# Two graph layers and a state-space scan: the three 128x1024 instructions that end the softplus move from GpSimd to VectorE, and GpSimd's output-norm work goes behind its product 13

## The chip, the cores and the metric

The kernel runs on one core of a Trainium2 chip. The metric is the device time of one execution in microseconds (us); the figure of a kernel is the median of several executions.

## The reference, cut to what matters

There are two layers on 4096 nodes with 128 features and a dense 4096x4096 adjacency matrix `adj`. The first is a pair of graph networks: `adj @ x` and `adj @ x2`, each through three dense layers, merged, added to `x` and normalized. The second is a Mamba block on `relu(adj @ x @ gcn_w + gcn_b)`:

```python
xconv = sum((xpad[k:k + L] * conv_w[:, k] for k in range(D_CONV))) + conv_b
u = jax.nn.silu(xconv)
dbc = u @ w_xp
dt = jax.nn.softplus(dbc[:, :DT_RANK] @ w_dt + b_dt)
B = dbc[:, DT_RANK:DT_RANK + D_STATE]
C = dbc[:, DT_RANK + D_STATE:]
A = -jnp.exp(A_log)
dA = jnp.exp(dt[:, :, None] * A[None])
dBu = dt[:, :, None] * B[:, None, :] * u[:, :, None]

def step(hst, inp):
    dAt, dBut, Ct = inp
    hst = dAt * hst + dBut
    return (hst, hst @ Ct)
_, ys = lax.scan(step, jnp.zeros((D_INNER, D_STATE), h.dtype), (dA, dBu, C))
y = ys + u * D_skip
y = y * jax.nn.silu(z)
return y @ w_out
```

L is 4096, D_INNER is 256 (two halves of 128 partitions) and D_STATE is 16. The result is added to the input and normalized once more.

## The kernel before, in words

**Stage A** (the first 515 us or so) turns `adj`, multiplies it with both inputs and stores the turned matrix. The change doesn't touch it.

**The scan stage** works on eight tiles of 512 nodes. One tile's turn is a window (`window(b, ...)`, one function of that name on each engine), numbered 0 to 7 here. A window has 16 steps n, one for each of the 16 states, and two more on VectorE for what trails behind. Each engine has its own program written out in order; engines meet only at semaphores, and an engine stops at a wait. Windows 2 and 3, then 4 and 5, are two passes of a loop of two iterations.

For state n of tile b there are four pieces of work:
- ScalarE makes `dA` (two exponentials of `dt`, L678);
- `dBu` is `dtu` times row n of B. For even n VectorE makes it as `dBuV` from a spread of B in PSUM (L898). For odd n GpSimd makes it as `dBuP` from `b_sb` in SBUF (L484, "product n" in the text), once scan n-3 is done;
- VectorE scans: `hs = dA * hs + dBu` over 1026 elements (L912, "scan n"), at its step n+1;
- VectorE multiplies `hs` with the spread of C in PSUM into `pr` (L919, "pr n"), at its step n+2; TensorE sums the `pr` up in `yT` (L1147). TensorE also makes the spreads of B and C (L1134 and L1143), turns, projects, and multiplies blocks of the stored adjacency for tile b+2 (L1063).

Beside this, window b does the **front** of tile b+1 (convolution, projections, softplus) and the **tail** of tile b-1 (gate, projection, output norm). The table `AT` gives the step of each such piece.

The softplus is made as relu + log(1 + exp(-abs)) with a correction of the rounding of 1 + exp. ScalarE makes the pieces at its steps 12 and 13. VectorE makes the error `sp_a` at its step 12 (`front_spd`, L868). Then come three instructions on 128x1024 floats, all with both inputs in SBUF: `sp_r = sp_r - sp_a` (L460), `dt = dt + sp_r` (L465), `dtu = dt * u` (L468). Before the change these three are `front_dt` on GpSimd, at its steps 13, 14 and 15 (`pool_dt=13`): one behind product 13, one in front of product 15, one behind it. For tile 0 VectorE makes them itself ahead of window 0 (L943, L946, L948).

The output norm of tile b-1: VectorE takes statistics at step 11 (`tail_stats`, L880 to L889), GpSimd makes `rs2` and `nb2` (`tail_rs`, L473 and L475, 4 columns each) at its step 12, between products 11 and 13, and ScalarE applies them at step 14.

In window b+1, VectorE's first instruction (`dBuV` of state 0) waits for `dtu`, and GpSimd's product 1 waits for `dtu` and for the last scan of window b. The gate (`tail_gate`, L874) stands at VectorE's step 1 of the window.

Of the kernel before, what the change touches and what calls it, by code (L numbers as in the profile page):

```python
# [7 lines left out]
ALU = mybir.AluOpType  # L8
# [23 lines left out]
def wait(eng, sem, value):  # L32

    if not isinstance(value, int) or value > 0:
# [1 line left out]

AT = dict(pool_rs=3, pool_tail_rs=12, pool_dt=13, act_hn=4, act_hT=5, act_silu=9, act_bc=11,
          act_sp=12, act_exp=13, act_tail=14, dve_g=1, dve_bc=9, dve_sp=12, dve_gate=1, dve_tail=11, pe_tr=3,  # L40
          pe_z=7, pe_dbc=8, pe_dt=10, pe_turn=2, pe_out=9, act_b0=14, act_b1=2, act_b2=5, act_b3=9, act_ax=15, act_g=0, act_start=1, act_skip=2, act_y=4)
FILL = (1, 1, 6, 1, 0, 0, 2, 9, 12)
# [9 lines left out]
def gnn_mamba(nc, x, adj, x2, eps1, eps2, W1, b1, W2, b2, Wm, bm, gcn_w, gcn_b, ln_g, ln_b, w_in, conv_w,  # L52
# [3 lines left out]
    with ctx:  # L56
# [311 lines left out]
        def _(pool):  # L368
# [85 lines left out]
                pool.wait_ge(f_inv_dev, a + 1)  # L454
                nc.gpsimd.tensor_tensor(nb[:, :], mr[:, :], rs[:, :], ALU.mult).then_inc(f_mean_scaled, 1)

            def front_dt(a, par, step):
                if step == 0:
                    pool.wait_ge(sp_error, a + 1)
                    nc.gpsimd.tensor_tensor(sp_r[:, :, :], sp_r[:, :, :], sp_a[:, :, :], ALU.subtract)\  # L460
                        .then_inc(sp_corrected, 1)
                elif step == 1:
                    pool.wait_ge(sp_corrected, a + 1)
                    pool.wait_ge(sp_log, a + 1)
                    nc.gpsimd.tensor_tensor(dt_[par][:, :, :], dt_[par][:, :, :], sp_r[:, :, :], ALU.add).then_inc(dt_ready, 1)  # L465
                else:
                    pool.wait_ge(dt_ready, a + 1)
                    nc.gpsimd.tensor_tensor(dtu[par][:, :, :], dt_[par][:, :, :], u[par][:, :, :], ALU.mult)\  # L468
                        .then_inc(dtu_ready, 1)

            def tail_rs(b):
                pool.wait_ge(o_var_eps, b + 1)
                nc.gpsimd.tensor_tensor(rs2[:, :], ve2[:, :], neg_half[:, :], ALU.pow).then_inc(o_inv_dev, 1)  # L473
# [3 lines left out]
            def window(b, par, tail, front):  # L477
                for n in range(S):
                    if n in POOL_B:
                        pair = nB(n) // 2  # L480
                        pool.wait_ge(b_in[pair % 2], 16 * (NPB // 4 * b + pair // 2 + 1))
                        wait(pool, scanned, S * b + (n - POOL_AFTER if n >= POOL_AFTER else -1) + 1)
                        pool.wait_ge(dtu_ready, b + 1)
                        nc.gpsimd.tensor_tensor(dBu(n, par)[:, :, 1:], dtu[par][:, :, :],  # L484
                                                b_sb[pair % 2][:, nB(n) % 2:nB(n) % 2 + 1, :].to_broadcast([P, H, TILE]),
                                                ALU.mult).then_inc(dBu_by_pool, 1)
                    if front and n == AT['pool_rs']:
                        front_rs(b + 1)
                    if tail and n == AT['pool_tail_rs']:
                        tail_rs(b - 1)  # L490
                    if front and 0 <= n - AT['pool_dt'] < 3:
                        front_dt(b + 1, 1 - par, n - AT['pool_dt'])

            front_rs(0)
            stage_a_over(pool)
# [253 lines left out]
        def _(dve):  # L749
# [116 lines left out]
            def front_spd(a, par):  # L866
                dve.wait_ge(sp_one_plus, a + 1)
                nc.vector.scalar_tensor_tensor(sp_a[:, :, :], dtu[par][:, :, :], -1.0, sp_a[:, :, :], ALU.add, ALU.subtract)\  # L868
                    .then_inc(sp_error, 1)

            def tail_gate(b, par):
                dve.wait_ge(summed, S * (b + 1))
                dve.wait_ge(gate_ready, 2 * b + 2)
                nc.vector.tensor_tensor(yg[:, :, :].rearrange("p q d -> p (q d)"), yT[:, :],  # L874
                                        sz[par][:, :, :].rearrange("p q d -> p (q d)"), ALU.mult).then_inc(y_gated, 1)
# [15 lines left out]
            def window(b, par, tail, front):  # L891
                for n in range(S + 2):
                    if n < S and n not in POOL_B:
                        dve.wait_ge(B_spread, NVB * b + n - nB(n) + 1)
                        if n == 0:
                            dve.wait_ge(dtu_ready, b + 1)
                        wait(dve, scanned, S * b + n - 1)
                        nc.vector.tensor_tensor(dBuV[dve_slot(n, par)][:, :, 1:], dtu[par][:, :, :],  # L898
                                                spread_bank("B", n)[:, :].unsqueeze(1).to_broadcast([P, H, TILE]), ALU.mult)\
                            .then_inc(dBu_by_dve, 1)  # L900
                    k = n - 1
                    if 0 <= k < S:
                        dve.wait_ge(dA_ready, H * (S * b + k + 1))
                        if k in POOL_B:
                            dve.wait_ge(dBu_by_pool, NPB * b + nB(k) + 1)
                        else:
                            dve.wait_ge(dBu_by_dve, NVB * b + k - nB(k) + 1)
                        wait(dve, state_kept, S * b + k - NHS + 1)
                        wait(dve, C_multiplied, S * b + k - NHS + 1)
                        dve.wait_ge(start_set, S * b + k + 1)  # L910
                        flat = [a[:, :, :].rearrange("p h t -> p (h t)") for a in (hs[k % NHS], dA[k % NDA], dBu(k, par))]
                        nc.vector.tensor_tensor_scan(flat[0], flat[1], flat[2], zero[:, :], ALU.mult, ALU.add)\  # L912
                            .then_inc(scanned, 1)
                    k = n - 2
                    if k >= 0:
                        dve.wait_ge(C_spread, S * b + k + 1)
                        dve.wait_ge(scanned, S * b + k + 1)
                        wait(dve, summed, S * b + k - NPR + 1)
                        nc.vector.tensor_tensor(pr[k % NPR][:, :, :], hs[k % NHS][:, :, 1:],  # L919
                                                spread_bank("C", k)[:, :].unsqueeze(1).to_broadcast([P, H, TILE]), ALU.mult)\  # L920
                            .then_inc(C_multiplied, 1)
                    if tail and n == AT['dve_gate']:
                        tail_gate(b - 1, 1 - par)
                    if front:
                        if n == AT['dve_g']:
                            front_g(b + 1)
                        if n == AT['dve_bc']:
                            front_bclo(b + 1, 1 - par)
                        if n == AT['dve_sp']:
                            front_spd(b + 1, 1 - par)  # L930
                    if tail:
                        if n == AT['dve_tail']:
                            tail_stats(b - 1, 1 - par)
# [5 lines left out]
            front_bclo(0, 0)  # L939
            front_spd(0, 0)  # L940

            dve.wait_ge(sp_error, 1)
            nc.vector.tensor_tensor(sp_r[:, :, :], sp_r[:, :, :], sp_a[:, :, :], ALU.subtract).then_inc(sp_corrected, 1)  # L943
            dve.wait_ge(sp_corrected, 1)
            dve.wait_ge(sp_log, 1)
            nc.vector.tensor_tensor(dt_[0][:, :, :], dt_[0][:, :, :], sp_r[:, :, :], ALU.add).then_inc(dt_ready, 1)  # L946
            dve.wait_ge(dt_ready, 1)
            nc.vector.tensor_tensor(dtu[0][:, :, :], dt_[0][:, :, :], u[0][:, :, :], ALU.mult).then_inc(dtu_ready, 1)  # L948
            dve.wait_ge(zeroed, 2 + NDA)
            window(0, 0, False, True)  # L950
            window(1, 1, True, True)
# [337 lines left out]
```

## Time and profile before

| what | value |
|---|---|
| median of 3 executions | 1172.0 us (1171.23 to 1174.01) |
| the profiled execution's own time | 1173.02 us |
| its span | 1171.5 us |
| VectorE (DVE) busy | 1053.3 us, 90% |
| TensorE (PE) busy | 1000.2 us, 85% |
| ScalarE (ACT) busy | 514.9 us, 44% |
| GpSimd (POOL) busy | 336.1 us, 29% |
| granted TensorE clock, mean of the span | 0.938 |

How to read it: the profile is one execution. Its span goes from the first to the last instruction, and its own time lies 1.5 us above that. An engine's busy time counts the time from an instruction's start to its end, also where the instruction stands still inside that time, so a stalled instruction looks like work. In a timeline row the first number is the start in us from the span's start, the second the length in us; what stands in square brackets is the engine's idle time before it and what ended it. Neighbours on VectorE overlap by about a tenth of a us, so what an instruction takes of the engine is the distance from its start to the next start.

### The profile page before, as it was taken

The numbers are of one execution on the slowest core, as the hardware profiler recorded it, in microseconds if no ns is written. First come the engines' busy times: TensorE is split into PE (matmuls) and PEld (weight loads), VectorE is DVE, ScalarE is ACT, GpSimd is POOL, SyncE is SP. The second block draws the span as 40 slices with busy tenths as digits, with TensorE's granted clock in tenths as the row PEclk, the third lists the DMA queues.
The fourth block names the chain that finished last, engine by engine and source line by source line (L and its number), as shares of the span: only waits on it lengthen the run. The fifth ranks groups of instructions, "written<-read, shape, count | busy, mean of one in ns | idle before, by whom it ended". The sixth has DMA issues, their size and how long they took to land. (4 is left out here: it accounts for less than half of the span.)

```text
span 1171.5 us, 13291 instructions
## 1 busy us (share of the span) xinstructions
PE 1000.2 (85%) x4162; PEld 691.5 (59%) x4162; DVE 1053.3 (90%) x864; ACT 514.9 (44%) x914; POOL 336.1 (29%) x207
## 2 busy tenths in 40 slices
PE   2789999999999999999988979889889798684565
PEld 1567776767777777444645646546556465463454
DVE  5899999999999998723999999999999999999994
ACT  3334334333334332225555655636456446565331
POOL 5100101000000001002354273463642734627340
PEclk9999999999999999999998989999989899895766
DMA  9989999999999999846444253253441542101100
GB/s 260 250 176 323 319 319 335 321 327 316 340 301 348 303 334 285 163 179 260 155 168 152 79 198 144 85 194 138 158 166 55 197 143 73 37 20 54 36 10 10
DMA packets 190907, 226.37 MB, mean 193 GB/s; under 512 B 8624, under 2 KB 164336, under 8 KB 176528
## 3 DMA queue, kind: packets, MB, share of 16 engines
q1 hardware_dynamic: 107008, 165.69, 44.2%
q10 hardware_dynamic: 80768, 52.70, 18.1%
q0 software_dynamic: 3088, 7.47, 2.3%
q8 instruction: 18, 0.29, 0.1%
q14 instruction: 25, 0.20, 0.1%
HBM read 162.66 MB, written 63.18 MB: 193 GB/s over the span
## 5 line engine op out<-in xcount | busy, mean ns | idle before, releaser
L771 DVE STREAM_TRANSPOSE at<-rows 128x1024 f32<-128x1024 f32 x136 | 267.2, 2005 | 24.9 <-DMA rows<-in_adj 14.2
L976 PE MATMUL yT<-ah,xh 128*128 128x512 f32 x512 | 214.4, 419 | 52.9 <-DVE al L779 52.9
L484 POOL TENSOR_TENSOR dBuP<-dtu,b_sb 128x1024 f32<-128x1024 f32 x64 | 167.2, 2613 | 256.8 <-DVE hs L912 193.8
L525 ACT ACTIVATE ah<-at 128x2048 fp32r<-128x2048 f32 x64 | 122.4, 1913 | 241.3 <-PE yT L976 231.1
L1063 PE MATMUL bank<-adjc,xm 128*128 128x512 f32 x448 | 213.6, 606 | 0.8 <-ACT axT L589 0.8
L976 PE MATMUL yT<-al,xh 128*128 128x512 f32 x512 | 202.0, 394 | 0.0
L976 PE MATMUL yT<-ah,xl 128*128 128x512 f32 x512 | 201.9, 394 | 0.0
L1147 PE MATMUL yT<-ident,pr 128*128 128x128 f32 x1024 | 159.3, 309 | 23.5 <-DVE pr L919 23.4
L912 DVE TENSOR_TENSOR_SCAN hs<-dA,zero,dBuP 128x1026 f32<-128x1026 f32 x64 | 166.3, 2598 | 8.4 <-ACT dA L678 8.4
L678 ACT ACTIVATE dA<-dt,A_sb 128x512 f32<-128x512 f32 x256 | 169.5, 713 | 9.2 <-POOL dt L465 6.5
L1147 PEld LDWEIGHTS yT<-ident,pr 128*128 128x128 f32 x1024 | 141.4, 162 | 48.8 <-DVE pr L919 33.2
L919 DVE TENSOR_TENSOR pr<-hs,bank 128x1024 f32<-128x1024 f32 x128 | 152.7, 1198 | 8.5 <-PE bank L1143 8.2
L912 DVE TENSOR_TENSOR_SCAN hs<-dA,zero,dBuV 128x1026 f32<-128x1026 f32 x64 | 157.8, 2466 | 1.6 <-DVE dBuV L898 1.2
L976 PEld LDWEIGHTS yT<-ah,xh 128*128 128x128 f32 x512 | 97.6, 191 | 88.0 <-DVE al L779 64.3
L779 DVE TENSOR_TENSOR al<-at,ah 128x2048 fp32r<-128x2048 f32 x64 | 144.3, 2254 | 0.2
L1063 PEld LDWEIGHTS bank<-adjc,xm 128*128 128x128 f32 x448 | 82.2, 197 | 71.1 <-issue 70.0
L976 PEld LDWEIGHTS yT<-ah,xl 128*128 128x128 f32 x512 | 97.7, 191 | 23.9 <-issue 5.0
L976 PEld LDWEIGHTS yT<-al,xh 128*128 128x128 f32 x512 | 97.5, 190 | 21.4
L1143 PE MATMUL bank<-bc,sel 128*128 128x512 f32 x128 | 87.1, 680 | 26.9 <-DVE pr L919 24.5
L428 POOL TENSOR_TENSOR ve<-mv,eps_ln 128x4 f32<-128x4 f32 x8 | 1.6, 195 | 326.8 <-DVE mv L796 326.8
L898 DVE TENSOR_TENSOR dBuV<-dtu,bank 128x1024 f32<-128x1024 f32 x64 | 77.8, 1215 | 1.7 <-issue 1.1
L671 ACT ACTIVATE state<-hs 128x2 f32<-128x2 f32 x128 | 25.7, 201 | 111.5 <-DVE hs L912 108.3
(147 smaller groups left out, 1027.1 us busy)
## 6 DMA issues: line engine op xcount, KB each, us to landing
adjT<-at SPq DMA_DIRECT2D x56, 1024.0 KB, 7.7
adjc<-adjT SPq DMA_DIRECT2D x56, 1024.0 KB, 5.1
rows<-in_adj SPq DMA_DIRECT2D x152, 256.0 KB, 8.6
rows<-in_adj ACTq DMA_DIRECT2D x136, 256.0 KB, 8.7
b_sb<-b_dram ACTq DMA_DIRECT2D x32, 512.0 KB, 3.8
xm<-in_x SPq DMA_DIRECT2D x4, 512.0 KB, 15.3
xs<-in_L_gnn_x SPq DMA_DIRECT2D x4, 512.0 KB, 14.7
res<-in_x POOLq DMA_DIRECT2D x8, 256.0 KB, 7.6
```

Of the source, the lines that this page charges most:

```text
L484: nc.gpsimd.tensor_tensor(dBu(n, par)[:, :, 1:], dtu[par][:, :, :], b_sb[pair % 2][:, nB(n) % 2:nB(n) % 2 + 1, :].to_broadcast([P, H, TILE ...
L525: nc.scalar.activation(ah[c % 2][:, :], at[c % 2][:, :, :].rearrange("p m t -> p (m t)"), ACT.Copy)\
L678: nc.scalar.activation(dA[n % NDA][:, h, 1:], dt_[par][:, h, :], ACT.Exp, scale=A_sb[:, h, n:n + 1]).then_inc(dA_ready, 1)
L771: last = nc.vector.transpose(dst.rearrange("p m (g i) -> p g m i", i=32), src.rearrange("p g (i m) -> p g m i", i=32))
L779: nc.vector.tensor_tensor(al[c % 2][:, :], at[c % 2][:, :, :].rearrange("p m t -> p (m t)"), ah[c % 2][:, :], ALU.subtract).then_inc(chunk ...
L898: nc.vector.tensor_tensor(dBuV[dve_slot(n, par)][:, :, 1:], dtu[par][:, :, :], spread_bank("B", n)[:, :].unsqueeze(1).to_broadcast([P, H, ...
L912: nc.vector.tensor_tensor_scan(flat[0], flat[1], flat[2], zero[:, :], ALU.mult, ALU.add)\
L919: nc.vector.tensor_tensor(pr[k % NPR][:, :, :], hs[k % NHS][:, :, 1:], spread_bank("C", k)[:, :].unsqueeze(1).to_broadcast([P, H, TILE]), ...
L976: last = mm(acc[k][:, :], w[:, b, :], v[c % 2][:, cols], start=(b == 0 and j == 0), stop=(b == KB - 1 and j == 2))
L1063: last = mm(accB[:, :], xm[:, b, :], adjc[c % NADJ][:, m, :], start=(b == 0), stop=(b == KB - 1))
L1143: mm(spread_bank("C", n)[:, :], sel[:, S + n:S + n + 1].to_broadcast([P, P]), bc[par][:, :], start=True, stop=True).then_inc(C_spread, 1)
L1147: m = mm(yT[:, DI * q + P * h:DI * q + P * h + P], src[:, h, P * q:P * q + P], ident[:, :], is_transpose=True, start=first and h == 0 and ...
```

## The change

Three edits:
- `front_dt` moves from GpSimd to VectorE, with its three instructions, waits and semaphores as they were. It stands at VectorE's steps 14, 15 and 16 (`dve_dt=14`), behind `pr` of that step.
- GpSimd's `tail_rs` goes from step 12 to step 13 (`pool_tail_rs=13`), that is from in front of product 13 to behind it.
- For tile 0, VectorE's own three instructions are now the same function; their order and waits are the same.

```diff
-AT = dict(pool_rs=3, pool_tail_rs=12, pool_dt=13, act_hn=4, act_hT=5, act_silu=9, act_bc=11,
+AT = dict(pool_rs=3, pool_tail_rs=13, dve_dt=14, act_hn=4, act_hT=5, act_silu=9, act_bc=11,
...
-            def front_dt(a, par, step):
-                if step == 0:
-                    pool.wait_ge(sp_error, a + 1)
-                    nc.gpsimd.tensor_tensor(sp_r[:, :, :], sp_r[:, :, :], sp_a[:, :, :], ALU.subtract)\
-                        .then_inc(sp_corrected, 1)
-                elif step == 1:
-                    pool.wait_ge(sp_corrected, a + 1)
-                    pool.wait_ge(sp_log, a + 1)
-                    nc.gpsimd.tensor_tensor(dt_[par][:, :, :], dt_[par][:, :, :], sp_r[:, :, :], ALU.add).then_inc(dt_ready, 1)
-                else:
-                    pool.wait_ge(dt_ready, a + 1)
-                    nc.gpsimd.tensor_tensor(dtu[par][:, :, :], dt_[par][:, :, :], u[par][:, :, :], ALU.mult)\
-                        .then_inc(dtu_ready, 1)
...
-                    if front and 0 <= n - AT['pool_dt'] < 3:
-                        front_dt(b + 1, 1 - par, n - AT['pool_dt'])
...
+            def front_dt(a, par, step):
+                if step == 0:
+                    dve.wait_ge(sp_error, a + 1)
+                    nc.vector.tensor_tensor(sp_r[:, :, :], sp_r[:, :, :], sp_a[:, :, :], ALU.subtract).then_inc(sp_corrected, 1)
+                elif step == 1:
+                    dve.wait_ge(sp_corrected, a + 1)
+                    dve.wait_ge(sp_log, a + 1)
+                    nc.vector.tensor_tensor(dt_[par][:, :, :], dt_[par][:, :, :], sp_r[:, :, :], ALU.add).then_inc(dt_ready, 1)
+                else:
+                    dve.wait_ge(dt_ready, a + 1)
+                    nc.vector.tensor_tensor(dtu[par][:, :, :], dt_[par][:, :, :], u[par][:, :, :], ALU.mult).then_inc(dtu_ready, 1)
...
+                        if 0 <= n - AT['dve_dt'] < 3:
+                            front_dt(b + 1, 1 - par, n - AT['dve_dt'])
```

**GpSimd at the end of window 1.** The rows go from the norm's two small instructions to the last instruction of the window. Each product is a row that writes `dBuP0` (product 13) or `dBuP1` (product 15). Before:

```order
L473 TENSOR_TENSOR rs2<-ve2,neg_half 128x4
L475 TENSOR_TENSOR nb2<-mr2,rs2 128x4
L484 TENSOR_TENSOR dBuP0<-dtu1,b_sb1 128x2x512
L460 TENSOR_TENSOR sp_r<-sp_r,sp_a 128x1024
L465 TENSOR_TENSOR dt0<-dt0,sp_r 128x1024
L484 TENSOR_TENSOR dBuP1<-dtu1,b_sb1 128x2x512
L468 TENSOR_TENSOR dtu0<-dt0,u0 128x1024
```

and now:

```order
L470 TENSOR_TENSOR dBuP0<-dtu1,b_sb1 128x2x512
L459 TENSOR_TENSOR rs2<-ve2,neg_half 128x4
L461 TENSOR_TENSOR nb2<-mr2,rs2 128x4
L470 TENSOR_TENSOR dBuP1<-dtu1,b_sb1 128x2x512
```

Product 13 no longer stands behind the two norm instructions, and product 15 no longer behind `sp_r` and `dt`.

**VectorE at the end of window 1**, from `sp_a` to the last `pr`. Rows that write `hs0` to `hs3` are scans 12 to 15; rows that write `pr3`, `pr0`, `pr1`, `pr2`, `pr3` are pr 11 to 15. Before:

```order
L868 SCALAR_TENSOR_TENSOR sp_a<-dtu0,sp_a 128x1024
L912 SCALAR_TENSOR_TENSOR hs0<-dA0,zero,dBuV0 128x1026
L919 TENSOR_TENSOR pr3<-hs3,bank5 128x1024
L898 TENSOR_TENSOR dBuV1<-dtu1,bank6 128x2x512
L912 SCALAR_TENSOR_TENSOR hs1<-dA1,zero,dBuP0 128x1026
L919 TENSOR_TENSOR pr0<-hs0,bank5 128x1024
L912 SCALAR_TENSOR_TENSOR hs2<-dA2,zero,dBuV1 128x1026
L919 TENSOR_TENSOR pr1<-hs1,bank6 128x1024
L912 SCALAR_TENSOR_TENSOR hs3<-dA3,zero,dBuP1 128x1026
L919 TENSOR_TENSOR pr2<-hs2,bank5 128x1024
L919 TENSOR_TENSOR pr3<-hs3,bank6 128x1024
```

and now, from scan 13 on:

```order
L908 SCALAR_TENSOR_TENSOR hs1<-dA1,zero,dBuP0 128x1026
L915 TENSOR_TENSOR pr0<-hs0,bank5 128x1024
L858 TENSOR_TENSOR sp_r<-sp_r,sp_a 128x1024
L908 SCALAR_TENSOR_TENSOR hs2<-dA2,zero,dBuV1 128x1026
L915 TENSOR_TENSOR pr1<-hs1,bank6 128x1024
L862 TENSOR_TENSOR dt0<-dt0,sp_r 128x1024
L908 SCALAR_TENSOR_TENSOR hs3<-dA3,zero,dBuP1 128x1026
L915 TENSOR_TENSOR pr2<-hs2,bank5 128x1024
L865 TENSOR_TENSOR dtu0<-dt0,u0 128x1024
L915 TENSOR_TENSOR pr3<-hs3,bank6 128x1024
```

One of the three stands behind each of pr 12, pr 13 and pr 14. What comes before scan 13 is as it was. ScalarE, TensorE and the DMA queues keep their order.

## Rows read from the trace of the kernel before

**Rows 1.** The page: busy time, share of the span, instructions, by engine.
```profile
PE 1000.2 (85%) x4162; PEld 691.5 (59%) x4162; DVE 1053.3 (90%) x864; ACT 514.9 (44%) x914; POOL 336.1 (29%) x207
```
**Rows 2.** Waits of VectorE, 515 to 1172 us: total us, times, longest us.
```profile
DVE hs L912 <- ACT dA L678: 8.4, 7, 1.5
DVE pr L919 <- PE bank L1143: 8.2, 16, 1.1
```
**Rows 3.** Timeline of VectorE, end of window 2 and start of window 3.
```profile
755.60 2.39 DVE L868 SCALAR_TENSOR_TENSOR sp_a<-dtu,sp_a 128x1024 f32<-128x1024 f32 x1
757.91 2.34 DVE L912 TENSOR_TENSOR_SCAN hs<-dA,zero,dBuV 128x1026 f32<-128x1026 f32 x1
760.18 1.19 DVE L919 TENSOR_TENSOR pr<-hs,bank 128x1024 f32<-128x1024 f32 x1
761.29 1.21 DVE L898 TENSOR_TENSOR dBuV<-dtu,bank 128x1024 f32<-128x1024 f32 x1
762.42 2.34 DVE L912 TENSOR_TENSOR_SCAN hs<-dA,zero,dBuP 128x1026 f32<-128x1026 f32 x1
...
765.80 3.28 DVE L912 TENSOR_TENSOR_SCAN hs<-dA,zero,dBuV 128x1026 f32<-128x1026 f32 x1
769.00 1.19 DVE L919 TENSOR_TENSOR pr<-hs,bank 128x1024 f32<-128x1024 f32 x1
771.34 4.37 DVE L912 TENSOR_TENSOR_SCAN hs<-dA,zero,dBuP 128x1026 f32<-128x1026 f32 x1 [1.15 <-ACT dA L678]
775.63 2.32 DVE L919 TENSOR_TENSOR pr<-hs,bank 128x1024 f32<-128x1024 f32 x2
777.87 1.21 DVE L898 TENSOR_TENSOR dBuV<-dtu,bank 128x1024 f32<-128x1024 f32 x1
779.37 2.36 DVE L912 TENSOR_TENSOR_SCAN hs<-dA,zero,dBuV 128x1026 f32<-128x1026 f32 x1 [0.29 <-DVE dBuV L898]
781.64 1.20 DVE L874 TENSOR_TENSOR yg<-yT,sz 128x1024 f32<-128x1024 f32 x1
```
**Rows 4.** Timeline of GpSimd, the same stretch.
```profile
752.32 2.24 POOL L475 TENSOR_TENSOR nb<-mr,rs 128x4 f32<-128x4 f32 x1
754.52 2.38 POOL L484 TENSOR_TENSOR dBuP<-dtu,b_sb 128x1024 f32<-128x1024 f32 x1
758.07 4.35 POOL L460 TENSOR_TENSOR sp_r<-sp_r,sp_a 128x1024 f32<-128x1024 f32 x1 [1.16 <-DVE sp_a L868]
762.50 4.43 POOL L465 TENSOR_TENSOR dt<-dt,sp_r 128x1024 f32<-128x1024 f32 x1
766.88 4.36 POOL L484 TENSOR_TENSOR dBuP<-dtu,b_sb 128x1024 f32<-128x1024 f32 x1
771.19 2.37 POOL L468 TENSOR_TENSOR dtu<-dt,u 128x1024 f32<-128x1024 f32 x1
```
**Rows 5.** Timeline of VectorE, the three instructions for tile 0, first two.
```profile
537.44 1.22 DVE L943 TENSOR_TENSOR sp_r<-sp_r,sp_a 128x1024 f32<-128x1024 f32 x1
538.70 1.22 DVE L946 TENSOR_TENSOR dt<-dt,sp_r 128x1024 f32<-128x1024 f32 x1
```
**Rows 6.** Timeline of VectorE, window 0's `sp_a` and window 1's gate.
```profile
600.99 1.21 DVE L868 SCALAR_TENSOR_TENSOR sp_a<-dtu,sp_a 128x1024 f32<-128x1024 f32 x1
...
625.65 1.20 DVE L874 TENSOR_TENSOR yg<-yT,sz 128x1024 f32<-128x1024 f32 x1
```
**Rows 7.** Timeline of VectorE, scans 12 and 13 of window 7.
```profile
1136.19 3.45 DVE L912 TENSOR_TENSOR_SCAN hs<-dA,zero,dBuV 128x1026 f32<-128x1026 f32 x1
...
1141.81 2.48 DVE L912 TENSOR_TENSOR_SCAN hs<-dA,zero,dBuP 128x1026 f32<-128x1026 f32 x1
```
**Rows 8.** Timeline of TensorE, the last wait of window 4.
```profile
931.00 0.79 PE L1134 MATMUL bank<-bc,sel 128*128 128x512 f32 x1 [4.38 <-DVE pr L919]
```
**Rows 9.** Timeline of VectorE, pr 0 and pr 1 of window 5.
```profile
942.28 1.22 DVE L919 TENSOR_TENSOR pr<-hs,bank 128x1024 f32<-128x1024 f32 x1 [0.18 <-PE bank L1143]
...
946.82 1.22 DVE L919 TENSOR_TENSOR pr<-hs,bank 128x1024 f32<-128x1024 f32 x1 [1.06 <-PE bank L1143]
```
**Rows 10.** Stretches of 2 us: us, PE busy, granted clock, DMA share, GB/s.
```profile
932.00:934.00 2.00, 2.00 (x12) 0.50 0.00 0
```

More of the change, by code:

```diff
@@ L940, in _ @@
             front_spd(0, 0)
[L942 to L948, printed above, removed]
+            for step in range(3):
+                front_dt(0, 0, step)
             dve.wait_ge(zeroed, 2 + NDA)
```

## The prediction

> **What bounds the kernel now.** I read the page first, then VectorE's waits, then the timelines of VectorE and GpSimd side by side over one window's end, and TensorE's timeline last. The page gives VectorE 90% and GpSimd 29% [rows 1]. By that alone the change is wrong: it puts 21 instructions (three in each of windows 0 to 6) on the fullest engine and takes them from an idle one. VectorE hardly waits in the scan stage either; the two largest entries that come back from window to window are 8.4 us and 8.2 us [rows 2]. So VectorE bounds this stage, and the question is whether its busy time is work.
>
> It isn't. In the timeline the same scan takes 2.34 us, then 3.28 us, then 4.37 us [rows 3]. Put GpSimd's rows beside them [rows 4]. Its `dt` starts at 762.50, while scan 13 runs from 762.42 to 764.76, and is 4.43 us long: 764.76 plus 2.17 is its end, 766.93. Scan 14 starts at 765.80; 766.93 plus 2.15 is 769.08, its end. Product 15 starts at 766.88 and lasts 4.36 us: 769.08 plus 2.16 is its end, 771.24. Then scan 15 starts at 771.34 just behind `dtu` (771.19 to 773.56) and ends at 775.71, 2.15 us behind `dtu`. The reading that fits all four: a scan (two inputs in SBUF) and a GpSimd instruction on SBUF exclude each other, the later one stands still until the other is through, and both show the standstill as busy time. VectorE's `pr` and `dBuV` (one input in PSUM) run beside GpSimd unharmed: 1.19 and 1.21 us [rows 3] while `sp_r` is on. `sp_a`, again with two SBUF inputs, is 2.39 us long where product 13 (754.52 to 756.90) is still running [rows 3, 4], and 1.21 us in window 0, where the norm work that delays product 13 doesn't exist [rows 6].
>
> The 1.15 us of idle time ahead of scan 15 are put down to ScalarE's `dA`, but scan 15 also needs product 15, which ended at 771.24, 0.1 us ahead of the start [rows 3, 4]. I take it for the releaser. It is late because `sp_r` and `dt` stand in front of it.
>
> **The change part by part.**
>
> *Three instructions on VectorE.* Alone, `sp_r` on VectorE is 1.22 us long [rows 5]. What it takes of the engine I read from `dBuV`, as long (1.21) and followed by the next start after 762.42 - 761.29 = 1.13 us [rows 3]. The bound above is 1.26 us, the distance in tile 0, where each waits for the one before [rows 5]; in the window each has a scan and a `pr` in between, so its own wait is long over. The bound below is 1.11 us, a `pr` [rows 3]. 1.13 it is.
>
> *The stretch from `sp_a` to the gate.* Before, in window 2, it is 781.64 - 755.60 = 26.04 us [rows 3]. After, I add distances between starts: `sp_a` and the three moved ones 4 x 1.13 = 4.52; scans 12 to 15, 4 x 2.27 (760.18 - 757.91) = 9.08; pr 11 to 15, 5 x 1.11 (761.29 - 760.18) = 5.55; `dBuV` 14, 1.13; the next window's first `dBuV`, 1.50, since the scan behind it waits for it (779.37 - 777.87); that scan, 2.27. Together 24.05 us.
>
> *New collisions.* Product 15 now waits only for scan 12, which ends as pr 11 starts. From there to scan 13 it has 1.11 + 1.13 = 2.24 us and needs 2.38. Window 7 shows the price of just this meeting: scan 13 is 2.48 us instead of 2.34 [rows 7], 0.14 more. Product 1 of the next window waits for `dtu`, now made behind pr 14; it has 1.11 + 1.50 us until the next scan, so 0 to 0.15, and I take 0.1. The stretch is then 24.3 us and saves 1.74 us. Windows 1 to 6 have this shape: 6 x 1.74 = 10.4 us. The four moved starts of waiting instructions are covered: `sp_error` and `sp_log` are made before scan 12, and behind `dtu` only pr 15 stands, then `dBuV`, whose input is through.
>
> *Window 0* has no norm work, so `sp_a` isn't held: 625.65 - 600.99 = 24.66 us [rows 6], less 24.3 = 0.4 us saved.
>
> *`tail_rs` behind product 13.* Product 13 waits only for scan 10, which ends before the statistics on VectorE; its 2.38 us lie beside them and `dBuV` 12. That is what frees `sp_a` above. In window 7 there is no `sp_a`, and it is scan 12 that product 13 holds: 3.45 us against 2.34 [rows 7], so 1.1 us saved. `rs2` and `nb2` wait for VectorE's `ve2` as before and end when they did (754.56 in window 2 [rows 4]); ScalarE's norm doesn't see it. `nb2` stands still through scan 11 in both orders. Product 15, queued behind it now, isn't due until 760.2. Cost 0. Tile 0's function is the same code: 0. ScalarE's first `dA` of the next window needs `dt`, now made behind pr 13 and some 7 us ahead of the scan that uses it: 0.
>
> *What TensorE gives back.* At a window's end TensorE waits 4.38 us for pr 14 [rows 8]; then it works without a gap until the spread of C that pr 1 needs, 946.82 - 931.00 = 15.8 us later [rows 8, 9]. The clock granted in this stretch is 0.50, its lower level of 1.2 GHz, right behind that idle time [rows 10]. In window 5 VectorE waits 0.18 and 1.06 us at pr 0 and pr 1 for it [rows 9]; the pair stands in windows 1, 2 and 5 and is part of the 8.2 us [rows 2]. The moved `dtu` comes between pr 14 and pr 15, so TensorE's burst starts 1.13 us earlier as VectorE counts. Of 1.24 us a window, 1.1 go: 3 x 1.1 = 3.3 us. The lower bound is 0, if the burst is late for another reason; the upper is all 8.2 us, if the shorter idle time keeps the clock at 2.4 GHz and that helps the other waits too.
>
> *Sum:* 10.4 + 0.4 + 1.1 + 3.3 = 15.2 us. The profiled execution's own time of 1173.0 becomes 1157.8. It stands 1.0 us above the median of 1172.0, so I expect a median of 1156.8. A measurement of this kernel tells apart about 0.2%, 2.3 us.
>
> **Where I weigh a rule.** The rows give a product 2.38 us where nothing is in the way (754.52) and 4.36 us where a scan is on [rows 4]; I took the first. The Trainium skill (Perfetto Trace Analysis, GPSIMD Engine Instruction) says that GpSimd's spans are unreliable and that the spacing of starts should be used. By spacing, product 15 costs 771.19 - 766.88 = 4.31 us, and the sum would be that of rival 3 below.
>
> **The rivals.**
>
> 1. *The window ends gain, TensorE's burst doesn't.* The waits at pr 0 and pr 1 stay: 11.9 us gained, 1160.1 us. For it: they stand in only three windows, so they hang on when the clock rises. Against: 1.13 us of head start at either clock.
>
> 2. *TensorE becomes the bound in windows 1 to 5.* It is 85% busy [rows 1] and has no gap after the boundary; the shorter end would turn into waits at the next start. Left are window 0, one full window and window 7: 0.4 + 1.7 + 1.1 = 3.2 us, 1168.8 us. Against: 4.38 us idle in each window before that burst [rows 8], more than the 1.74 taken out.
>
> 3. *No change.* A product needs 4.3 us whatever VectorE does. Then product 15 ends 4.31 - 2.24 = 2.07 us late for scan 13, in seven windows: 14.5 us of the 15.2 are gone, 1171.3 us. Against: `sp_a` of 2.39 us ended 1.1 us behind a product of 2.38 us, as if that were its true end [rows 3, 4]. The Trainium skill (same page, Optimizing Scalar/DVE Operations) warns that moving work between these two engines may not help, because they share a read port.
>
> 4. *Slower: the moved instructions come in the way of GpSimd's products.* They too have two SBUF inputs. If product 15 started 1 us or more after scan 12's end, as it would if its data or `nb2` came late, it would run into scan 13, and the chain of standstills of [rows 3, 4] goes on, 1.1 us at scan 13 or 14 and 3.2 at scan 15. Of the old losses only `sp_a`'s 1.18 us come back, against 3.39 us of new work: 2.2 us more in six windows, 3.4 in window 0, less 1.1 in window 7: 15.5 us, 1187.5 us. It decides at 1 us of lateness; `nb2` ends 5.6 us early.
>
> **How the numbers follow.** The forecast, with TensorE's part between half and all of its 3.3 us and some clock gain, has 0.57. Rival 1 has 0.22, rival 2 0.10, rival 3 0.04, rival 4 0.05; 0.02 lie below the range. From below the range takes in 1172.0 - 11.9 - 8.2 = 1151.9. From above it takes rival 1 with the dear price of 1.26 us for the moved ones (21 x 0.13 = 2.7 us), 1162.8, and a little of rival 2: 1152 to 1164. Faster by over 0.2% are the forecast, what lies below the range, and rivals 1 and 2, 0.91; within 0.2% is rival 3, 0.04; slower is rival 4, 0.05.
>
> **What would show it.** Scans 14 and 15 of every window at 2.34 us; `sp_a` at 1.2 us in windows 1 to 6; no idle time ahead of scan 15; the three moved instructions at 1.2 us each; GpSimd's product 15 at 2.4 us, starting with pr 11; a stretch from `sp_a` to the gate of 24.3 us (25.4 in window 3, where the loop branches); the waits at pr 0 and pr 1 gone, DVE's total on TensorE's spreads near 5 us. I am wrong if a scan or a moved instruction is longer than 2.6 or 1.4 us, if product 15 runs through scan 13, or if VectorE's waits for TensorE grow by what the ends gain.

## The result, and the profile after

| kernel | median | executions | profiled execution: own time, span |
|---|---|---|---|
| before | 1172.05 us | 6, 1171.23 to 1174.36 | 1173.02, 1171.5 us |
| changed | 1153.97 us | 6, 1151.05 to 1161.63 | 1153.26, 1151.7 us |

The ratio is 0.985 (95% interval 0.982 to 0.988). The changed kernel is 18.1 us faster by the medians and 19.8 us by the two profiled executions. The forecast was 1156.8 us, 15.2 us faster.

The page of the changed kernel, busy times by engine:

```profile
PE 994.8 (86%) x4162; PEld 685.5 (60%) x4162; DVE 1048.3 (91%) x885; ACT 514.6 (45%) x914; POOL 249.8 (22%) x186
```

VectorE has 21 instructions more than in [rows 1] and is 5 us less busy. GpSimd is 86 us less busy, though its 21 instructions were 78 us on the page before and cost VectorE only 21 x 1.2; the rest is that the products, which stand still less, fell from 167.2 to 153.7 us, while the front norm's `nb` rose from 11.8 to 15.8 us.

VectorE at the end of window 2, timeline of the changed kernel (L852 is `sp_a`, L908 the scans, L915 `pr`, L858, L862 and L865 the moved three, L894 `dBuV`, L870 the gate):

```profile
749.81 1.22 DVE L852 SCALAR_TENSOR_TENSOR sp_a<-dtu,sp_a 128x1024 f32<-128x1024 f32 x1
750.95 2.35 DVE L908 TENSOR_TENSOR_SCAN hs<-dA,zero,dBuV 128x1026 f32<-128x1026 f32 x1
...
755.46 2.44 DVE L908 TENSOR_TENSOR_SCAN hs<-dA,zero,dBuP 128x1026 f32<-128x1026 f32 x1
757.82 1.19 DVE L915 TENSOR_TENSOR pr<-hs,bank 128x1024 f32<-128x1024 f32 x1
758.93 1.21 DVE L858 TENSOR_TENSOR sp_r<-sp_r,sp_a 128x1024 f32<-128x1024 f32 x1
760.06 2.34 DVE L908 TENSOR_TENSOR_SCAN hs<-dA,zero,dBuV 128x1026 f32<-128x1026 f32 x1
762.33 1.19 DVE L915 TENSOR_TENSOR pr<-hs,bank 128x1024 f32<-128x1024 f32 x1
763.44 1.21 DVE L862 TENSOR_TENSOR dt<-dt,sp_r 128x1024 f32<-128x1024 f32 x1
764.58 2.34 DVE L908 TENSOR_TENSOR_SCAN hs<-dA,zero,dBuP 128x1026 f32<-128x1026 f32 x1
766.85 1.18 DVE L915 TENSOR_TENSOR pr<-hs,bank 128x1024 f32<-128x1024 f32 x1
767.96 1.21 DVE L865 TENSOR_TENSOR dtu<-dt,u 128x1024 f32<-128x1024 f32 x1
...
771.72 2.36 DVE L908 TENSOR_TENSOR_SCAN hs<-dA,zero,dBuV 128x1026 f32<-128x1026 f32 x1 [0.29 <-DVE dBuV L894]
773.99 1.20 DVE L870 TENSOR_TENSOR yg<-yT,sz 128x1024 f32<-128x1024 f32 x1
```

Against [rows 3]: `sp_a` 1.22 instead of 2.39 us, scan 14 2.34 instead of 3.28, no idle time ahead of scan 15, and scan 15 2.34 instead of 4.37. From `sp_a` to the gate it is 24.18 us instead of 26.04.

GpSimd in the same stretch of the changed kernel, timeline (L470 is the product, L461 `nb2`):

```profile
742.78 2.39 POOL L470 TENSOR_TENSOR dBuP<-dtu,b_sb 128x1024 f32<-128x1024 f32 x1 [6.93 <-DVE hs L908]
...
746.53 2.25 POOL L461 TENSOR_TENSOR nb<-mr,rs 128x4 f32<-128x4 f32 x1
753.38 2.37 POOL L470 TENSOR_TENSOR dBuP<-dtu,b_sb 128x1024 f32<-128x1024 f32 x1 [4.60 <-DVE hs L908]
769.31 2.39 POOL L470 TENSOR_TENSOR dBuP<-dtu,b_sb 128x1024 f32<-128x1024 f32 x1 [13.56 <-DVE dtu L865]
```

Product 13 is through before the norm's work, and product 15 starts with pr 11 and takes 2.37 us instead of the 4.36 of [rows 4]. The row behind it is product 1 of window 3.

VectorE's waits for TensorE's spreads of C in the changed kernel (us in total, times, longest), 8.2 us and 16 times in [rows 2]:

```profile
DVE pr L915 <- PE bank L1136: 2.8, 7, 0.5
```

**Where the 19.8 us lie.** I cut the scan stage at each `sp_a` and each gate and subtract. The stretches from `sp_a` to the gate give 12.0 us over windows 0 to 6. The stretches from the gate to `sp_a`, windows 1 to 6, give 6.4 us: 51.8, 52.0, 50.6, 50.3, 52.0 and 49.5 us before, 50.1, 50.4, 50.7, 49.7, 49.4 and 49.5 after. Window 7 gives 1.35 us and what lies behind its end 0.15.

### The profile page after: what moved, and what is told of

It reads as the page before. It is cut to its first block and busy times, and to the rows that moved or that the text cites. A ratio compares the mean times of both kernels' runs of the same rounds, so it can differ in the third digit from the quotient of the medians.

```text
span 1151.7 us, 13291 instructions
## 1 busy us (share of the span) xinstructions
PE 994.8 (86%) x4162; PEld 685.5 (60%) x4162; DVE 1048.3 (91%) x885; ACT 514.6 (45%) x914; POOL 249.8 (22%) x186
## 5 line engine op out<-in xcount | busy, mean ns | idle before, releaser
L470 POOL TENSOR_TENSOR dBuP<-dtu,b_sb 128x1024 f32<-128x1024 f32 x64 | 153.7, 2402 | 399.4 <-DVE hs L908 231.4
L1056 PE MATMUL bank<-adjc,xm 128*128 128x512 f32 x448 | 209.4, 596 | 0.8 <-ACT axT L573 0.8
L1140 PE MATMUL yT<-ident,pr 128*128 128x128 f32 x1024 | 155.7, 303 | 32.6 <-DVE pr L915 32.5
L1140 PEld LDWEIGHTS yT<-ident,pr 128*128 128x128 f32 x1024 | 135.0, 157 | 60.5 <-DVE pr L915 46.6
L915 DVE TENSOR_TENSOR pr<-hs,bank 128x1024 f32<-128x1024 f32 x128 | 152.8, 1194 | 3.0 <-PE bank L1136 2.8
L908 DVE TENSOR_TENSOR_SCAN hs<-dA,zero,dBuP 128x1026 f32<-128x1026 f32 x64 | 154.0, 2406 | 0.0
L908 DVE TENSOR_TENSOR_SCAN hs<-dA,zero,dBuV 128x1026 f32<-128x1026 f32 x64 | 150.2, 2347 | 1.6 <-DVE dBuV L894 1.2
L894 DVE TENSOR_TENSOR dBuV<-dtu,bank 128x1024 f32<-128x1024 f32 x64 | 77.7, 1214 | 1.2 <-issue 0.9
```

Of the source, the lines that this page charges most:

```text
L1056: last = mm(accB[:, :], xm[:, b, :], adjc[c % NADJ][:, m, :], start=(b == 0), stop=(b == KB - 1))
L1140: m = mm(yT[:, DI * q + P * h:DI * q + P * h + P], src[:, h, P * q:P * q + P], ident[:, :], is_transpose=True, start=first and h == 0 and ...
```

## The experiments

Twelve kernels. "Before" and "changed" mean the two kernels above.

**1. Only the three instructions move.** Edit on the changed kernel:

```diff
-AT = dict(pool_rs=3, pool_tail_rs=13, dve_dt=14, ...
+AT = dict(pool_rs=3, pool_tail_rs=12, dve_dt=14, ...
```

> The three softplus instructions on VectorE alone; GpSimd's norm work stays in front of product 13. Theory (two-input instructions on VectorE and GpSimd exclude each other): sp_a is 2.4 us long again in windows 1 to 6 and scan 12 of window 7 is 3.45 us, so against the changed kernel 6 x 1.16 + 1.1 = 8.1 us are lost, while scans 14 and 15 stay at 2.34 us: about 1162 us. Rival (the two edits only work together, because product 15 is late without the second): scans 13 to 15 are stretched too, 1175 us or more.

Measured: 1159.8 us (1159.1 to 1164.5), ratio to before 0.990 (0.988 to 0.993). VectorE's timeline of that kernel, `sp_a` and scans 12 to 15 of window 2:

```profile
749.88 2.39 DVE L852 SCALAR_TENSOR_TENSOR sp_a<-dtu,sp_a 128x1024 f32<-128x1024 f32 x1
752.19 2.34 DVE L908 TENSOR_TENSOR_SCAN hs<-dA,zero,dBuV 128x1026 f32<-128x1026 f32 x1
...
756.70 2.43 DVE L908 TENSOR_TENSOR_SCAN hs<-dA,zero,dBuP 128x1026 f32<-128x1026 f32 x1
...
761.30 2.35 DVE L908 TENSOR_TENSOR_SCAN hs<-dA,zero,dBuV 128x1026 f32<-128x1026 f32 x1
...
765.82 2.34 DVE L908 TENSOR_TENSOR_SCAN hs<-dA,zero,dBuP 128x1026 f32<-128x1026 f32 x1
```

`sp_a` alone is long, the scans are not; scan 12 of window 7 is 3.45 us again. The theory holds, the rival (the edits only work together) falls. The stretches from `sp_a` to the gate and window 7 lose the forecast 8.1 us, but the whole only 5.9 by the profiled executions (1157.6 against 1151.7 us of span). The stretches from the gate to `sp_a` give 2.5 us back: 297.3 us in sum where the changed kernel has 299.8, and VectorE waits once, 0.2 us, for a spread of C. The clock fell here too. Granted clock ahead of the gate at 775.23 us, in stretches of 2 us (us, PE busy, granted clock, DMA share, GB/s):

```profile
770.00:772.00 2.00, 2.00 (x10) 0.50 0.06 24
772.00:774.00 2.00, 2.00 (x13) 0.76 0.00 0
774.00:776.00 2.00, 2.00 (x7) 1.00 0.00 0
```

TensorE waits 2.33 us for pr 14 up to 769.33 us, as long as in the changed kernel, and the clock is back 1.2 us ahead of the gate; in the changed kernel it is at 0.55 in the last 2 us ahead of its gate (run 4 shows the rows). The changed kernel's next wait of TensorE, 0.89 us for pr 15, isn't there in run 1. My reading is that the slow stretch falls into that wait; why it comes earlier here, no run tells.

**2. Only the norm's work moves.** On the kernel before, `pool_tail_rs=12` becomes 13.

> Only GpSimd's norm work goes behind product 13; the three softplus instructions stay on GpSimd. Theory: sp_a is 1.2 us in windows 1 to 6, window 7's scan 12 is 2.34 us, but scans 14 and 15 are stretched as before: 1172.0 - 8.1 = 1164 us. Rival (GpSimd's chain is the thing that sets the window's end, and it starts at product 13): sp_r starts earlier and scan 15 is no longer stretched, 1158 us or less.

Measured: 1163.3 us (1161.7 to 1164.3), ratio 0.991 (0.990 to 0.993). VectorE's timeline of that kernel, `sp_a`, scan 14 and scan 15 of window 2:

```profile
752.41 1.22 DVE L868 SCALAR_TENSOR_TENSOR sp_a<-dtu,sp_a 128x1024 f32<-128x1024 f32 x1
...
761.43 3.29 DVE L912 TENSOR_TENSOR_SCAN hs<-dA,zero,dBuV 128x1026 f32<-128x1026 f32 x1
...
766.97 4.37 DVE L912 TENSOR_TENSOR_SCAN hs<-dA,zero,dBuP 128x1026 f32<-128x1026 f32 x1 [1.14 <-ACT dA L678]
```

The mirror image: `sp_a` is short, scans 14 and 15 are as long as before. Each edit removes its own meetings. In the runs of these two, before had a median of 1173.4 us; against that the edits alone are worth 13.6 and 10.1 us. Together they gave 18.1 us in the runs of the result (19.5 against 1173.4 us), so 4 to 6 us are counted twice. In the profiles the double count lies where VectorE waits for TensorE: the stretches from the gate to `sp_a` give 8.8 and 2.9 us alone and 6.4 together, those from `sp_a` to the gate 5.1 and 6.0 alone and 12.0 together. TensorE's burst, its work behind its wait for pr 14 ("TensorE's last wait" here), is what the next two runs are about.

**3. The moved instructions in front of `pr`.** Edit on the changed kernel:

```diff
                             .then_inc(scanned, 1)
+                    if front and 0 <= n - AT['dve_dt'] < 3:
+                        front_dt(b + 1, 1 - par, n - AT['dve_dt'])
                     k = n - 2
...
-                        if 0 <= n - AT['dve_dt'] < 3:
-                            front_dt(b + 1, 1 - par, n - AT['dve_dt'])
```

> As the changed kernel, but each of the three moved instructions stands in front of the pr of its step, not behind it. VectorE has the same work and no new collision. Theory (head start for TensorE): pr 14 comes 1.13 us later as VectorE counts, TensorE waits some 3.5 us for it instead of 2.3, its burst is late again, and the waits at pr 0 and pr 1 and part of those at pr 6 and pr 8 come back: 1154 + 3.3 to 6.4 = 1157 to 1160 us. Rival (the waits went because the whole window got shorter): no difference, 1154 us.

Measured: 1154.7 us (1153.4 to 1156.4), ratio 0.984 (0.983 to 0.986). By the time alone this is the rival. The waits say otherwise; the row of that kernel:

```profile
DVE pr L917 <- PE bank L1136: 6.0, 15, 0.5
```

The waits came back, from 2.8 to 6.0 us: every stretch from the gate to `sp_a` in windows 1 to 5 is 50.7 or 50.8 us. Two things hid it. The stretch across the loop's branch, windows 3 to 4, fell from 25.15 to 24.23 us, so the branch's 0.9 us lie beside something in this order; why, no run tells. And TensorE's last wait did not grow to 3.5 us as I wrote but stayed at 2.32, since its work before that wait hangs on pr 13, which comes later too. The six stretches from the gate to `sp_a` are 3.3 us longer in these profiles (303.1 against 299.8 us), but that is not all the head start: 1.3 us lie in window 5, ahead of which the changed kernel's clock did not fall (920 to 924 us) and this one's did, and 1.1 in window 4, where the branch on VectorE gives the changed kernel's TensorE 0.9 us more. In window 1 the dips are alike (0.55 and 0.59 in the 4 us from 620 us in the changed kernel, 0.60 and 0.55 here), and there the head start is worth 0.6 us. So it is real and small.

**4. TensorE's last wait filled.** Edit on the changed kernel (the products are read by nothing, and their bank is free there):

```diff
+                    if adj_ and n == S:
+                        for _ in range(2):
+                            mm(accB[:, :], w_cv_sb[:, 0, 0, :], hT[:, TAPS - 1:], start=True, stop=True)
                     if front and n == S:
                         spread_B(b + 1, 0, 1 - par)
```

> As the changed kernel, with two 512-column float products into a free bank in front of TensorE's last wait of windows 0 to 5 (extra work, read by nothing). Theory (the low clock behind TensorE's idle time costs the rest of the waits): the granted clock stays at 1.00 across the boundaries of windows 0 to 5, VectorE's waits for TensorE's spreads of C fall from 2.8 us to under 1 us, 1 to 3 us gained: 1151 to 1153 us. Rival (TensorE is short of time there, not of clock): the 1.8 us of added work delay its burst, and the waits grow by up to 1 us a window: 1157 to 1160 us.

Measured: 1150.8 us (1150.2 to 1152.7), ratio 0.982 (0.980 to 0.983). Granted clock behind the boundary of windows 2 and 3 in stretches of 2 us (us, PE busy, granted clock, DMA share, GB/s), the changed kernel first:

```profile
770.00:772.00 2.00, 1.65 (x8) 0.60 0.00 0
772.00:774.00 2.00, 2.00 (x8) 0.55 0.00 0
```

and the filled one, where the gate comes 1.44 us earlier:

```profile
768.00:770.00 2.00, 1.11 (x11) 1.00 0.00 1
770.00:772.00 2.00, 2.00 (x10) 1.00 0.00 0
```

VectorE has no wait for a spread of C left, and all five stretches from the gate to `sp_a` in windows 1 to 5 are 49.4 or 49.5 us. TensorE does more work and the kernel is 3.1 us faster. What kept four of the changed kernel's five stretches at 49.7 to 50.7 us was TensorE's clock at its lower level of 1.2 GHz behind 2.33 us of idle time. The fifth, ahead of which the clock stayed up, has 49.4 us there too. The rival falls. The Trainium skill (TensorE: Matmul & The Clock Gate, What's actually happening) says that the slow clock is the default and activity releases it; this pair of runs agrees.

**5 and 6. Two more GpSimd instructions, reading or only writing.** Edit on the changed kernel, behind product 15 of windows 0 to 6 (beside it a scratch tile `scr`, set once ahead of window 0, and two semaphores of its own); in the second run the product is `memset(scr[:, :], 0.0)`:

```diff
+                    if front and n == 15:
+                        for j in range(2):
+                            pool.wait_ge(scr_set, 2 * b + j + 1)
+                            pool.sem_inc(scr_seen, 1)
+                            nc.gpsimd.tensor_tensor(scr[:, :], w_in_sb[:, 0:416], w_in_sb[:, 0:416], ALU.mult).then_inc(scr_set, 1)
```

> As the changed kernel, with two more GpSimd instructions of 416 columns in each window from 0 to 6, right behind product 15: products of two SBUF operands into a scratch tile that nothing reads. Theory (a GpSimd instruction that reads SBUF and a VectorE instruction with two SBUF inputs exclude each other): the first stands still until scan 13 is through, the second runs into sp_r, which then is about 2.1 us long instead of 1.2: 7 x 0.9 = 6 us more, 1160 us. Rival (the long scans came from the order of the semaphores, not from a shared resource): nothing waits for the two, so 1154 us.

> The same place and the same 416 columns, but the two added GpSimd instructions are memsets, which read nothing. Theory (the exclusion is of reads): scan 13, sp_r and scan 14 keep 2.44, 1.21 and 2.34 us; 1154 us. Rival (any GpSimd work on SBUF beside a VectorE instruction with two SBUF inputs holds it): scan 13 or sp_r is stretched, as in the run with products, 1157 to 1160 us.

Measured: 1158.9 us (1157.1 to 1160.4), ratio 0.988 (0.986 to 0.990), with products; 1153.5 us (1153.2 to 1155.2), ratio 0.984 (0.983 to 0.986), with memsets. GpSimd's timeline with products:

```profile
757.39 2.87 POOL L483 TENSOR_TENSOR scr<-w_in_sb 128x416 f32<-128x416 f32 x1
760.43 0.88 POOL L483 TENSOR_TENSOR scr<-w_in_sb 128x416 f32<-128x416 f32 x1 [0.17 <-POOL scr L483]
```

VectorE's, scan 13 and `sp_r` of the same window:

```profile
757.14 2.44 DVE L916 TENSOR_TENSOR_SCAN hs<-dA,zero,dBuP 128x1026 f32<-128x1026 f32 x1
...
760.62 1.77 DVE L866 TENSOR_TENSOR sp_r<-sp_r,sp_a 128x1024 f32<-128x1024 f32 x1
```

GpSimd's timeline with memsets, and VectorE's `sp_r` there:

```profile
755.70 0.45 POOL L483 MEMSET scr<- 128x416 f32 x1
756.30 0.44 POOL L483 MEMSET scr<- 128x416 f32 x1
```

```profile
758.96 1.21 DVE L866 TENSOR_TENSOR sp_r<-sp_r,sp_a 128x1024 f32<-128x1024 f32 x1
```

A product of 416 columns takes 0.88 us alone and 2.87 us when scan 13 is on: it ends 0.68 us behind it. The second runs into `sp_r`, which is 0.56 us longer, in each of seven windows. Nothing waits for either product, so no semaphore made this. The memsets lie inside scan 13 (755.48 to 757.92 there), run their 0.45 us, and cost nothing. So it is GpSimd's reading that excludes a VectorE instruction with two SBUF inputs. `sp_r` gives 7 x 0.56 = 3.9 of the 4.9 us by medians; I had expected 0.9 a window. The changed kernel's own executions scatter by more than 4.9 us; against the kernel with memsets, whose executions don't overlap with these, the products cost 5.4 us.

**7 and 8. Filled in other places.** Run 7 joins runs 3 and 4, with three products instead of two. Run 8 is the filled kernel with this in window 7:

```diff
+                    if not front and n >= 10:
+                        for _ in range(2):
+                            mm(accB[:, :], w_cv_sb[:, 0, 0, :], hT[:, TAPS - 1:], start=True, stop=True)
```

> The two edits together: each moved instruction in front of the pr of its step, and three added products on TensorE in front of its last wait. With the moved ones in front, the loop branch between windows 3 and 4 was hidden (0.9 us) and the waits for TensorE came back (6.0 us in all). Theory (those waits are the low clock's): filled, they vanish here too, and the time is that of the filled kernel less the branch: 1150 us. Rival (they are the lost head start's): about 3 us more than the filled kernel, 1154 us.

> The filled kernel with two more added products on TensorE in each of the last seven steps of window 7. Theory (the kernel's last chain, 15.5 us from the last gate to the end, runs at the low clock: sums, turns, projection): the granted clock is 1.00 from the middle of window 7 on, the wait of the last gate shrinks from 2.3 to about 1.5 us and the projection's matmuls by 2 us: 1148 us. Rival (the chain idles too much to keep the clock, or the added work delays pr): no gain or up to 3 us lost, 1151 to 1154 us.

Measured: run 7 1150.3 us (1147.4 to 1151.3), ratio 0.980 (0.978 to 0.982). No wait for a spread of C is left, and the stretches are 49.4 us although the head start is missing: with the clock up, it isn't needed. Run 8 1149.7 us (1148.7 to 1149.8), ratio 0.981 (0.979 to 0.982), between the two expectations: in its profile the wait of the last gate fell from 2.27 to 1.68 us, but the clock fell again behind it, so the projection ran slow.

**9. One of the three left out.** VectorE leaves out `sp_r = sp_r - sp_a` and only passes its semaphore on.

> As the changed kernel, but VectorE leaves out the first of the three moved instructions, sp_r = sp_r - sp_a, in all tiles (the correction of the softplus is then off by sp_a). Theory (a moved instruction takes 1.13 us of VectorE and all of it lies on the path): 8 x 1.13 = 9 us less, 1145 us, with the stretch from sp_a to the gate 1.13 us shorter. Rival (TensorE is now close behind, so that shorter ends come back as waits): 3 us or more of the 9 turn into waits at pr, 1148 us or more.

Measured: 1146.7 us (1144.3 to 1153.5), ratio 0.981 (0.977 to 0.984): 7.3 us less than the changed kernel by medians, 9.0 by the spans (1142.7 against 1151.7). Every stretch from `sp_a` to the gate is 1.13 us shorter (23.05 in window 2; 1.33 across the branch, which cost less), and the stretches from the gate to `sp_a` are 0.6 us longer in sum. A moved instruction takes 1.13 us and is wholly on the path. The scatter of 9 us leaves the share that comes back in other executions open.

**10. Product 15 late.** Edit on the changed kernel:

```diff
-                        wait(pool, scanned, S * b + (n - POOL_AFTER if n >= POOL_AFTER else -1) + 1)
+                        wait(pool, scanned, S * b + (13 if n == 15 else n - POOL_AFTER if n >= POOL_AFTER else -1) + 1)
```

> As the changed kernel, but GpSimd's product 15 waits for scan 13 where it waited for scan 12, in all windows. This is what rival 4 of the prediction needs. Theory (one meeting, then apart): product 15 starts with pr 12, sp_r behind it stands still for about 1.25 us and is 2.5 us long, scan 15 has its input in time: 7 x 1.25 - 7 x 0.1 = 8 us more, 1162 us. Rival (a chain of standstills as in the kernel before): sp_r, scan 14 and scan 15 are all stretched, 2.2 us or more a window, 1169 to 1187 us.

Measured: 1161.1 us (1160.7 to 1161.7), ratio 0.991 (0.989 to 0.993). VectorE's timeline of window 2, scan 13 to scan 15, and GpSimd's product 15 below:

```profile
758.00 2.35 DVE L908 TENSOR_TENSOR_SCAN hs<-dA,zero,dBuP 128x1026 f32<-128x1026 f32 x1
760.27 1.20 DVE L915 TENSOR_TENSOR pr<-hs,bank 128x1024 f32<-128x1024 f32 x1
761.38 2.50 DVE L858 TENSOR_TENSOR sp_r<-sp_r,sp_a 128x1024 f32<-128x1024 f32 x1
763.80 2.34 DVE L908 TENSOR_TENSOR_SCAN hs<-dA,zero,dBuV 128x1026 f32<-128x1026 f32 x1
...
768.32 2.34 DVE L908 TENSOR_TENSOR_SCAN hs<-dA,zero,dBuP 128x1026 f32<-128x1026 f32 x1
```

```profile
760.43 2.37 POOL L470 TENSOR_TENSOR dBuP<-dtu,b_sb 128x1024 f32<-128x1024 f32 x1 [9.10 <-DVE hs L908]
```

One meeting, 1.3 us, and no chain; in window 7, which has no `sp_r`, it is scan 14 that takes 3.61 us. That a chain needs several GpSimd instructions one behind the other, as the kernel before had, fits these rows and is not tested by itself.

**11. All that helped.** Run 7 and the filling of run 8 together.

> Everything that helped: the moved instructions in front of the pr of their step, three added products on TensorE at the boundaries of windows 0 to 5 and two in each of the last seven steps of window 7. Theory (the branch of the loop, the boundary waits and the last chain are separate costs): the filled end's 1149.7 us less 0.8 for the branch, 1149 us. Rival (they overlap, or the branch's place depends on the run): no better than 1149.7 us.

Measured: 1145.7 us (1145.6 to 1146.1), ratio 0.978 (0.976 to 0.980), the fastest full computation of this study. It is 3.3 us better than I expected. TensorE's projection at its end, timeline:

```profile
1133.22 0.49 PE L1171 MATMUL bank<-res,ident 128*128 128x128 f32 x2 [0.74 <-ACT y L640]
1133.55 0.61 PE L1173 MATMUL bank<-w_out_sb,y 128*128 128x128 f32 x4
```

In the changed kernel the same two groups were

```profile
1139.28 0.80 PE L1171 MATMUL bank<-res,ident 128*128 128x128 f32 x2 [0.74 <-ACT y L640]
1139.87 1.06 PE L1173 MATMUL bank<-w_out_sb,y 128*128 128x128 f32 x4
```

Here the clock held through the last chain, 1.00 in every stretch of 2 us from 1112 to 1140 us, where in run 8 it fell to 0.64 and 0.51 behind the last gate. Its executions lie within 0.5 us; those of the changed kernel lie 10.6 us apart.

**12. The kernel before, filled.** The edit of run 4 with three products, on the kernel before.

> The kernel before, with none of the two edits, and three added products on TensorE in front of its last wait of windows 0 to 5, which leave about 1.6 us of its 4.4 us idle. Theory (the stretches from the gate to sp_a were long because TensorE's burst ran at the low clock, and the head start of the change was only one way out): every such stretch of windows 1 to 5 is 49.4 us, 9.6 us in sum off the kernel before, with the scans of 3.28 and 4.37 us left as they are: 1163 us. Rival (without the head start the burst stays late at either clock): half of it or less, 1167 us or more.

Measured: 1165.9 us (1164.1 to 1167.7), ratio 0.994 (0.992 to 0.996), 7.4 us less than before in the same runs. Four of the five stretches are 49.4 us; at the boundary of windows 2 and 3 the clock fell all the same, and the stretch behind it is 50.7. The time lies between the expectations; the five stretches give 8.4 of the expected 9.6 us, and the end behind the last gate is 1.1 us longer than before. So the theory holds where it applies: without any head start the waits go where the clock stays up. The scans of 3.28 and 4.38 us are all there.

## Why the prediction was right, and where it was short

The median is 2.8 us under the forecast. The sum was made for the profiled execution, and there it fell 4.6 us short: 15.2 us forecast, 19.8 measured. 3.1 of these are TensorE's term, 1.2 the stretches from `sp_a` to the gate, and 0.4 window 7 and its end. Every term came out at its forecast or above, so no error covers another.

**What bounds it.** Right. The stalls inside VectorE's instructions were work only by name. Runs 5 and 6 show the exclusion by itself; for its reading from the four rows they are the proof that the prediction didn't have.

**The moved instructions, 1.13 us each.** Right: 1.13 between starts, and 1.13 a window in run 9.

**The stretch from `sp_a` to the gate.** Forecast 24.3 us and 1.74 saved; measured 24.18 and 1.86 in window 2. Scan 13 meets product 15 for 0.10 us (0.14 forecast); product 1's 0.1 us against the next window's first scan didn't come, that scan is 2.36 us. Over windows 0 to 6 this term was 10.8 us and came out as 12.0.

**`tail_rs` behind product 13.** Right in both places: `sp_a` at 1.22 us, `nb2` as late as before with respect to its scan, and window 7 1.35 us shorter (1.1 forecast). Run 1 takes it away again: 25.35 us for the stretch.

**What TensorE gives back.** The mechanism was there and the size was wrong: 3.3 us forecast, 6.4 in the profiled pair. This is the step that failed, "Of 1.24 us a window, 1.1 go". It counted only the two waits at pr 0 and pr 1 in windows 1, 2 and 5, 3.7 of the 8.2 us, gave the waits of 0.46 us further on in the windows no term, and named the clock only as an upper bound. They hang on the same thing: run 4 has none of them. Both causes are at work. With the clock's dips alike, taking the head start away costs 0.6 us a window (window 1 of run 3); holding the clock up takes away all the rest (runs 4 and 7) and does most of it on the kernel before, with no head start at all (run 12). It isn't the fall alone that counts but when it comes: in run 1 the clock fell at every boundary and VectorE waited 0.2 us in all. In the profiled pair window 5 gives 2.6 of the 6.4 us, and the clock didn't fall ahead of it; run 3, where it did, has 50.7 us in that window, so 1.3 of the 2.6 hang on a fall that failed to come. The prediction had no reason for that, and so far its gain is luck.

**The rivals.** Rival 1 (ends only, 1160.1 us) and rival 2 (TensorE as the bound) fell: VectorE's waits for TensorE shrank from 8.2 to 2.8 us. Rival 3 fell: product 15 takes 2.37 us when nothing is in its way, and its 14 us weren't lost. GpSimd's reported spans and VectorE's stalls fit together to 0.1 us here once the standstill is counted. The rule of the Trainium skill (Perfetto Trace Analysis, GPSIMD Engine Instruction) to use the spacing of starts would have led astray in this kernel. Rival 4 fell; run 10 shows that with product 15 late the price against the forecast is about 7 us and not 30.

## What to carry to other kernels

Before an engine at 90% is spared by moving work off it, compare the lengths of one kind of instruction: a scan that is 2.34 us here and 4.37 us there is waiting, and here 21 short instructions on the full engine took away longer stalls than they cost. A GpSimd instruction that reads SBUF and a VectorE instruction with two SBUF inputs took turns wherever they met here: put GpSimd's reads beside VectorE's instructions with a PSUM operand, and no two of them in a row. An engine that waits shortly in front of its burst can lose by its clock what the wait itself doesn't cost; filling that wait with products that nothing reads was worth 3 us here at no cost to the path.

## What the runs showed of the hardware that I had not expected

- TensorE idle for 2.33 us at a window's end had its clock at 0.60 and 0.55 in the next 4 us in some windows and at 1.00 in others of the same execution (920 to 924 us of the changed kernel); with 0.61 us left of that wait in run 4 it stayed at 1.00 behind the ends of all the filled windows.
- GpSimd's memset of 416 columns ran its 0.45 us in the middle of a scan, with neither slowed; its product of 416 columns took 2.87 us in place of 0.88.
- VectorE's loop branch cost 0.5 to 1.2 us between windows 3 and 4 in most kernels, 2.2 us in run 2, and 0.1 to 0.3 us where `dtu` stood in front of pr 14 (runs 3, 7 and 11). What hides it there is open.
